# Routing of a mixture-of-experts layer: logits computed turned with the gate held in TensorE, and one-hot matrices built in bf16 for sixteen columns at once

## The chip, the cores and the metric

The kernel runs on one core of one Trainium2 chip. The metric is the device time of the whole program in microseconds (us), the median of repeated executions. TensorE (PE) multiplies, VectorE (DVE), ScalarE (ACT) and GpSimd (POOL) do the rest, SyncE (SP) issues most transfers.

## The reference

One macaron block over 4 × 1024 tokens of 256 channels, in float32:

```
x = x + 0.5 * ffn(layernorm(x))
x = x + attention(layernorm(x))      # 16 heads, RoPE, causal
x = x + 0.5 * ffn(layernorm(x))      # the same weights again

def ffn(x):                          # 4096 tokens, 8 experts, 2 of them for each token
    logits = x @ gate_w.T            # [4096, 8]
    top_w, sel = top_k(softmax(logits), 2); top_w /= sum(top_w)
    # each token: sum over its two experts of top_w * (silu(x @ w_gate[e]) * (x @ w_up[e])) @ w_down[e]
```

## The kernel before, in words

Everything runs in phases with a barrier between them: a setup, the first FFN (`ffn_phase`, tag f1), a projection phase, attention, an output phase, and `ffn_phase` again (tag f2). Each engine has one instruction list, written out by hand and run in order; semaphores are the only order between engines. The diff touches `ffn_phase` alone, and that runs twice. It has these stages.

**Logits stage.** The 4096 tokens are 32 tiles of 128. For each tile DVE normalises it (`normalise`, L386), SP stores it to DRAM (L312), PE turns it (two 128×128 transposes, `turn`, L567), ACT copies it out of PSUM (L520), and PE multiplies it with the gate (`logits`, L573): the turned tile is the stationary operand, and the eight columns of the gate move. `normalise(t)` needs the buffer of tile t−8, so it waits until that tile's store has landed (`xn_stored`) and until it is turned. In the same stage POOL splits the weights of the eight experts into a high and a low part (L336 to L341). Only two experts' raw weights fit, so SP, between two stores, waits for a split before it issues the next load: `load_weights(t // 5 + 2)` follows the store of tile 4, 9, 14, 19, 24 and 29, and waits until expert `t // 5` is split. The stores behind it in SP's queue wait with it.

**Choice and ranks.** DVE finds the two best experts of each token (`choose`, L401 to L405, and L409 between the two calls), PE counts tokens before each one, and DVE works out for each of the 8192 (token, choice) pairs a slot: a tile number `slot_j` (0 to 70) and a row `slot_p` (0 to 127).

**Inversion of the slots.** The experts need the reverse: which pair sits in a slot. The 8192 pairs are 64 columns of 128. For each column DVE writes a one-hot matrix of rows (L447, 128×128) and one of tiles times the pair number (L448, 128×71), both float32, and PE adds their product into `ps_owner` (L588), a float32 matmul that the chip runs as two passes. The buffers hold two lots of four columns. DVE then makes `pair_i` and `token_i` (L451 to L453), which release POOL's first gather, and a packed list of experts (L456 to L466), for which PE waits before the expert loop.

**Expert loop.** 71 tiles of 128 slots: gather by POOL, turn, gate and up, silu, down, scatter by POOL. After f2 the result is mixed into x and stored.

Of the kernel before, what the change touches and what calls it, by code (L numbers as in the profile page):

```python
# [18 lines left out]
BF16 = mybir.dt.bfloat16  # L19
# [13 lines left out]
SLOT_TILES = TOPK * NT + E - 1  # L33
DEEP = 8
# [10 lines left out]
                ("below", E), ("count", 128), ("pair1", TOPK * NT)]  # L45
# [6 lines left out]
def constants():  # L52
# [21 lines left out]
    put("pair1", TOPK * (P * np.arange(NT)[None, None, :] + p[:, None, None]) + np.arange(TOPK)[None, :, None] + 1)  # L74
# [83 lines left out]
def ffn_phase(nc, tag, cst, x_sb, rstd, nmr, w_mix, gate_sb, w_gate, w_up, w_down, xn_dram, y_dram, spare, out):  # L158
# [3 lines left out]
    with Semaphores(nc) as sems, ctx:  # L162
# [31 lines left out]
        xnT = carve(P, 4, KD, P)  # L194
# [28 lines left out]
        slot_j = sb("slot_j", [P, TOPK * NT])  # L223
        slot_p = sb("slot_p", [P, TOPK * NT])

        carved[0] = xnT_at
        at_row = carve(P, 2, 4, P)
        at_tile = carve(P, 2, 4, SLOT_TILES)
        empty = sb("empty", [P, SLOT_TILES])
        pair_i = sb("pair_i", [P, SLOT_TILES], I32)  # L230
# [33 lines left out]
        stats_own, moments = sem("stats_own"), sem("moments")  # L264
        xn_ready, xn_turned, xnT_ready, logits_done = sem("xn_ready"), sem("xn_turned"), sem("xnT_ready"), sem("logits_done")
# [111 lines left out]
        def _(dve):  # L377
# [3 lines left out]
            def normalise(t, u):  # L381
                if u == 0:
                    dve.wait_ge(moments, t // 8 + 1)
                wait(dve, xn_stored[u], 16 * (t // 8))
                wait(dve, xn_turned, t - 7)
                dve.tensor_scalar(xn[:, u, :], x_sb[:, t, :], rstd[:, t:t + 1], nmr[:, t:t + 1], ALU.mult, ALU.add).then_inc(xn_ready, 1)  # L386

            for t in range(NT):
                normalise(t, t % 8)
# [17 lines left out]
            dve.wait_ge(logits_done, NT)  # L407
# [34 lines left out]
            rows, tiles = cst("count"), cst("count")[:, 0:SLOT_TILES]  # L442
# [117 lines left out]
        def _(pe):  # L560
# [15 lines left out]
            for t in range(NT + 2):
                if t < NT:
                    turn(t)
                if t >= 2:
# [1054 lines left out]
```

## Time and profile before

| | |
|---|---|
| median of 3 runs | 1312.65 us (1310.78 to 1316.44) |
| the profiled execution | 1310.62 us, of which the span of its instructions is 1308.9 us |
| first FFN's logits stage | about 30.7 to 72.2 us |
| second FFN's logits stage | about 995.4 to 1037.2 us |
| second FFN: choice and ranks, inversion, expert loop and rest | 1037.2 to 1050.1, to 1078.3, to 1308.9 us |

Times in rows count from the first instruction. PEld is the weight load of TensorE, which overlaps PE. A duration on an engine holds a fixed latency that the next instruction may overlap, so what a stream costs is read from the distance of two starts. PEclk 1.00 is 2.4 GHz and 0.50 is 1.2 GHz.

### The profile page before, as it was taken

How to read it: one execution, taken by the hardware profiler on the slowest of the kernel's cores; microseconds unless marked ns; L12 is line 12 of the kernel's file. 1: busy time of each engine (PE TensorE's matmuls, PEld its weight loads, DVE VectorE, ACT ScalarE, POOL GpSimd, SP SyncE). 2: the span in 40 equal slices, each digit the busy share in tenths (PEclk: the TensorE clock that was granted, in tenths of full speed). 3: DMA queues.
4: the chain of work that ended last, by engine and by line, in shares of the span. 5: the costliest groups of instructions: out<-in, count | busy, mean ns of one | idle time of the engine just before them, and what ended most of it. 6: DMA issues, size and time to landing. Idle time of an engine off the chain costs nothing. (4 is left out here: it accounts for less than half of the span.)

```text
span 1308.9 us, 24181 instructions
## 1 busy us (share of the span) xinstructions
PE 1066.9 (82%) x6982; PEld 722.4 (55%) x6982; DVE 910.0 (70%) x2809; ACT 632.4 (48%) x1314; POOL 601.4 (46%) x757
## 2 busy tenths in 40 slices
PE   1958998890688659999999999999987788988850
PEld 1957987780576613333333333333286688977740
DVE  5787444444798768988999988898176894444436
ACT  1301555550576604666666666666762204555420
POOL 1923777773699801222222222222306707777750
PEclk9999999995799957999999999999986558999975
DMA  6611333321466531112111111100003402233339
GB/s 215 206 33 39 98 98 98 99 80 44 120 180 181 170 103 52 51 53 62 57 60 59 56 52 57 61 32 2 2 1 116 146 1 89 91 96 95 97 112 326
DMA packets 84077, 117.44 MB, mean 90 GB/s; under 512 B 11358, under 2 KB 64364, under 8 KB 80880
## 3 DMA queue, kind: packets, MB, share of 16 engines
q1 hardware_dynamic: 67200, 79.17, 19.3%
q0 software_dynamic: 13632, 33.59, 8.2%
q10 hardware_dynamic: 3120, 3.15, 0.7%
q8 instruction: 63, 1.03, 0.3%
q14 instruction: 62, 0.51, 0.1%
HBM read 75.48 MB, written 43.78 MB: 91 GB/s over the span
## 5 line engine op out<-in xcount | busy, mean ns | idle before, releaser
L1257 ACT ACTIVATE a_probs<-a_ps_s 128x1024 f32<-128x1024 f32 (+3 forms) x384 | 294.3, 813 | 173.1 <-PE a_ps_s L1289 171.9
L1172 POOL TENSOR_SCALAR_AFFINE_SELECT a_probs<-a_probs 128x256 f32<-128x256 f32 x256 | 102.5, 406 | 369.6 <-ACT a_probs L1257 366.9
L1190 DVE CUSTOM_DVE_ANT_0 a_unused<-a_ps_m,const_sb 128x128 bf16<-128x128 f32 (+3 forms) x512 | 234.1, 485 | 26.7 <-PE a_ps_m L1274 16.8
L1274 PE MATMUL a_ps_m<-st_k,st_q 96*128 96x512 bf16 (+3 forms) x768 | 219.7, 345 | 24.4 <-PEq L155 17.1
L354 POOL DMA_INDIRECT v_sb<-xn_dram,f_token_i x142 | 145.4, 1024 | 124.0 <-issue 80.5
L1192 DVE TENSOR_REDUCE a_max_a<-a_ps_m 128x1 f32<-128x512 f32 x256 | 175.7, 686 | 14.3 <-PE a_ps_m L1274 13.9
L1289 PE MATMUL a_ps_s<-st_q,st_k 98*128 98x512 bf16 (+3 forms) x768 | 180.8, 329 | 1.5 <-ACT a_probs L1257 1.4
L1274 PEld LDWEIGHTS a_ps_m<-st_k,st_q 96*128 96x128 bf16 x768 | 67.9, 98 | 196.6 <-DVE a_max_a L1192 55.9
L476 DVE TENSOR_TENSOR f_h<-f_ps_gu,f_sg 128x176 f32<-128x176 f32 x142 | 48.5, 341 | 175.3 <-ACT f_sg L537 175.3
L1302 PE MATMUL a_ps_ctx<-a_probs,a_v_st 128*32 128x512 f32 (+3 forms) x1536 | 163.7, 498 | 1.3 <-POOL a_probs L1172 0.6
L359 POOL DMA_INDIRECT y_dram<-v_sb,f_pair_i x142 | 143.5, 1011 | 43.5 <-issue 41.0
L1289 PEld LDWEIGHTS a_ps_s<-st_q,st_k 98*128 98x128 bf16 x768 | 65.4, 98 | 72.4 <-ACT a_probs L1257 42.6
L610 PE MATMUL f_ps_gu<-f_gu_hi,f_xT_hi 128*128 x284 | 95.9, 338 | 10.6 <-DVE f_xT_lo L471 9.8
L527 ACT ACTIVATE f_xT_hi<-f_ps_xT 128x256 fp32r<-128x256 f32 x142 | 53.6, 377 | 104.1 <-PE f_ps_xT L600 103.5
L628 PE MATMUL f_ps_y<-f_dn_hi,f_hT_hi 88*128 x284 | 92.9, 327 | 0.1
L610 PE MATMUL f_ps_gu<-f_gu_hi,f_xT_lo 128*128 x284 | 92.9, 327 | 0.0
L610 PE MATMUL f_ps_gu<-f_gu_lo,f_xT_hi 128*128 x284 | 92.9, 327 | 0.0
L537 ACT ACTIVATE f_sg<-f_ps_gu 128x176 f32<-128x176 f32 x142 | 45.0, 317 | 97.8 <-PE f_ps_gu L610 97.8
L600 PE MATMUL f_ps_xT<-const_sb,v_sb 128*128 128x128 f32 x284 | 59.2, 291 | 29.2 <-DMA v_sb<-xn_dram,f_token_i 28.9
L628 PE MATMUL f_ps_y<-f_dn_lo,f_hT_hi 88*128 x284 | 80.0, 282 | 0.0
L628 PE MATMUL f_ps_y<-f_dn_hi,f_hT_lo 88*128 x284 | 79.4, 280 | 0.0
L532 ACT ACTIVATE v_sb<-f_ps_y 128x256 f32<-128x256 f32 x142 | 54.6, 385 | 45.4 <-PE f_ps_y L628 45.4
(172 smaller groups left out, 2249.3 us busy)
## 6 DMA issues: line engine op xcount, KB each, us to landing
xn_dram<-v_sb SPq DMA_DIRECT2D x64, 128.0 KB, 3.4
p_yb<-y_dram SPq DMA_DIRECT2D x32, 256.0 KB, 2.8
v_sb<-y_dram SPq DMA_DIRECT2D x32, 256.0 KB, 3.8
st_q<-qk_dram SPq DMA_DIRECT2D x16, 384.0 KB
st_k<-qk_dram SPq DMA_DIRECT2D x16, 384.0 KB
qk_dram<-st_rT_hi SPq DMA_DIRECT2D x16, 256.0 KB, 2.9
qk_dram<-st_rT_mid SPq DMA_DIRECT2D x16, 256.0 KB, 3.5
qk_dram<-st_rT_lo SPq DMA_DIRECT2D x16, 256.0 KB, 5.1
```

The source lines that it names most:

```text
L354: pool.indirect_dma_start(xg[:, slot, :], None, xn_dram, bass.IndirectOffsetOnAxis(ap=token, axis=0), bounds_check=last_token, oob_is_err= ...
L359: pool.indirect_dma_start(y_dram, bass.IndirectOffsetOnAxis(ap=pair, axis=0), y_sb[:, slot, :], None, bounds_check=last_pair, oob_is_err=F ...
L600: mm = pe.transpose(ps_xT[b][:, k, :], xg[:, u, k * P:(k + 1) * P], ident)
L610: mm = pe.matmul(ps_gu[b][:, 0:2 * F], x_part[:, b, k, :], w_part[:, bass.ds(e, 1), k, :].rearrange("p a f -> p (a f)"), start=(n == 1), s ...
L628: mm = pe.matmul(ps_y[b][:], h_part[:, b, c, :], w_part[:, bass.ds(e, 1), c, :].rearrange("p a f -> p (a f)"), start=(n == 1), stop=(n == 6))
L1172: pool.affine_select(out=tri, in_=tri, compare_op=ALU.is_ge, fill=zero, base=0, pattern=[[0, 2], [1, P]], channel_multiplier=-1).then_inc( ...
L1190: dve.tensor_tensor_reduce(unused[:, bank, 0:nk], ps, cst("mask")[:, HALF - nk:HALF], 1.0, NEG, ALU.add, ALU.max, at).then_inc(taken, 1)
L1192: dve.tensor_reduce(at, ps, AX.X, ALU.max).then_inc(taken, 1)
L1257: act.activation(probs[:, s % 4, :, 0:nq], ps_s[s % 2][:, :, 0:nq], ACT.Exp, scale=float(HD) ** -0.5).then_inc(exp_done, 1)
L1274: pe.matmul(ps_m[bank][:, 0:nk], q_st[b][0:MAX_ROW, h, P * i:P * i + P], k_st[b][0:MAX_ROW, h, k0:k0 + nk], start=True, stop=True).then_in ...
L1289: mm = pe.matmul(ps_s[s % 2][:, n, 0:nq], k_st[b][:, h, P * j:P * j + P], q_st[b][:, h, q0:q0 + nq], start=True, stop=True)
L1302: mm = pe.matmul(ps_ctx[32 * h:32 * h + 32, q0 - HALF * half:HALF], v_st[b % 2][:, j, h, :], probs[:, (2 * v + h // 2) % 4, h % 2, 0:nq], ...
```

## The change

Three things. (1) `normalise` goes from DVE to ACT, and the copy of turned tiles from ACT to DVE; the gate becomes the stationary operand (128×8), four turned tiles (512 columns) move, DVE copies the 8×512 logits out of PSUM, and four small transposes bring them back to token rows. (2) The one-hot matrices are bf16 and built for sixteen columns by four DVE instructions, with a table `count_lot` that ACT writes once. (3) A pair number is no exact bf16 number, so the tile matrix has two halves of 71: 256 × tile number, and the low part; PE multiplies 142 columns in one bf16 pass, and one more DVE instruction adds the halves.

```
+LOT = 16
...
-        xnT = carve(P, 4, KD, P)
+        xnT = carve(P, 2, KD, 4 * P)
+        lgT = carve(E, 2, 4 * P)
...
+        count_lot = sb("count_lot", [P, P, LOT], BF16)
+        tile256 = sb("tile256", [P, TOPK * NT], BF16)
+        at_tile = sb("at_tile", [P, 2, 2 * SLOT_TILES, LOT], BF16)
-        at_row = carve(P, 2, 4, P)
-        at_tile = carve(P, 2, 4, SLOT_TILES)
+        at_row = carve(P, P * LOT).bitcast(BF16).rearrange("p (b s i) -> p b s i", b=2, s=P)
...
         @block.vector
-            def normalise(t, u):
...
+            def copy_turned(t):
+                i, u = t // 4, t % 4
+                dve.wait_ge(xn_turned, t + 1)
                 if u == 0:
+                    wait(dve, logits_done, i - 1)
+                dve.tensor_copy(xnT[:, i % 2, :, u * P:(u + 1) * P], ps_turn[u]).then_inc(xnT_ready, 1)
+
+            def copy_logits(i):
+                dve.wait_ge(logits_done, i + 1)
+                wait(dve, lg_ready, i - 1)
+                dve.tensor_copy(lgT[:, i % 2, :], ps_lgT[i % 2]).then_inc(lgT_ready, 1)
+
+            for i in range(NT // 4 + 1):
+                for u in range(4):
+                    if i < NT // 4:
+                        copy_turned(4 * i + u)
+                    if u == 1 and i > 0:
+                        copy_logits(i - 1)
...
-            for i in range(TOPK * NT):
-                b = i // 4 % 2
-                if i % 4 == 0:
-                    wait(dve, one_hot_used, i // 4 - 1)
-                dve.tensor_scalar(at_row[:, b, i % 4, :], rows, slot_p[:, i:i + 1], None, ALU.is_equal).then_inc(one_hot_ready, 1)
-                dve.tensor_scalar(at_tile[:, b, i % 4, :], tiles, slot_j[:, i:i + 1], cst("pair1")[:, i:i + 1],
-                                  ALU.is_equal, ALU.mult).then_inc(one_hot_ready, 1)
+            dve.wait_ge(count_ready, 2)
+            for lot in range(TOPK * NT // LOT):
+                b, of = lot % 2, slice(LOT * lot, LOT * (lot + 1))
+                hit, by_tile_no = at_tile[:, b, SLOT_TILES:2 * SLOT_TILES, :], at_tile[:, b, 0:SLOT_TILES, :]
+                per_tile = [P, SLOT_TILES, LOT]
+                wait(dve, one_hot_used, lot - 1)
+                own.then_wait(dve.tensor_tensor(hit, count_lot[:, 0:SLOT_TILES, :], slot_j[:, of].unsqueeze(1).to_broadcast(per_tile), ALU.is_equal))
+                own.then_wait(dve.tensor_tensor(by_tile_no, hit, tile256[:, of].unsqueeze(1).to_broadcast(per_tile), ALU.mult))
+                dve.tensor_scalar(hit, hit, cst("low")[:, LOT * lot // NT:LOT * lot // NT + 1], None, ALU.mult).then_inc(one_hot_ready, 1)
+                dve.tensor_tensor(at_row[:, b, :, :], count_lot[:], slot_p[:, of].unsqueeze(1).to_broadcast([P, P, LOT]),
+                                  ALU.is_equal).then_inc(one_hot_ready, 1)
...
+            own.then_wait(dve.tensor_tensor(pair_i[:], ps_owner[:, 0:SLOT_TILES], low[:], ALU.add))
...
         @block.scalar
+            def normalise(t, u):
+                if u == 0:
+                    act.wait_ge(moments, t // 8 + 1)
+                wait(act, xn_stored[u], 16 * (t // 8))
+                wait(act, xn_turned, t - 7)
+                act.activation(xn[:, u, :], x_sb[:, t, :], ACT.Identity, bias=nmr[:, t:t + 1], scale=rstd[:, t:t + 1]).then_inc(xn_ready, 1)
             for t in range(NT):
-                act.wait_ge(xn_turned, t + 1)
-                wait(act, logits_done, t - 3)
-                act.activation(xnT[:, t % 4, :, :], ps_turn[t % 4], ACT.Copy).then_inc(xnT_ready, 1)
+                normalise(t, t % 8)
+            act.activation(count_lot[:], cst("count").unsqueeze(2).to_broadcast([P, P, LOT]), ACT.Copy).then_inc(count_ready, 1)
+            act.activation(tile256[:], cst("tile256"), ACT.Copy).then_inc(count_ready, 1)
...
         @block.tensor
+            def logits(i):
+                pe.wait_ge(xnT_ready, 4 * i + 4)
+                wait(pe, lgT_ready, i - 1)
                 for k in range(KD):
+                    mm = pe.matmul(ps_lgT[i % 2], gate_sb[:, k, :], xnT[:, i % 2, k, :], start=(k == 0), stop=(k == KD - 1))
                 mm.then_inc(logits_done, 1)
+            def turn_back(i):
+                pe.wait_ge(lgT_ready, i + 1)
+                for u in range(4):
+                    mm = pe.transpose(ps_lg[:, 4 * i + u, :], lgT[:, i % 2, u * P:(u + 1) * P], ident[0:E, 0:E])
+                mm.then_inc(lg_ready, 1)
+
+            for i in range(NT // 4 + 2):
+                for u in range(4):
+                    if i < NT // 4:
+                        turn(4 * i + u)
+                    if u == 1 and 0 < i <= NT // 4:
+                        logits(i - 1)
+                if i >= 2:
+                    turn_back(i - 2)
...
             for i in range(TOPK * NT):
+                lot, b = i // LOT, i // LOT % 2
+                pe.wait_ge(one_hot_ready, 2 * lot + 2)
+                mm = pe.matmul(ps_owner, at_row[:, b, :, i % LOT], at_tile[:, b, :, i % LOT], start=(i == 0), stop=(i == TOPK * NT - 1))
```

## Rows read from the trace of the kernel before

**Rows 1.** The chain that ended last, in order of time, second FFN
```profile
1007.33 3.68 DMA xn_dram<-v_sb
...
1050.70 27.59 PE f_ps_y L588 x128
```

**Rows 2.** Stretches of both FFNs: length, busy of PE, PEld, DVE, ACT, POOL, PEclk, DMA
```profile
30.70:72.20 41.50, 38.58 (x192) 38.09 (x192) 29.06 (x34) 12.28 (x32) 38.36 (x37) 1.00 0.66 200
...
995.40:1037.20 41.80, 38.09 (x192) 37.85 (x192) 27.53 (x35) 12.29 (x32) 40.11 (x38) 0.50 0.65 199
1037.20:1050.10 12.90, 0.61 (x2) 0.13 (x2) 11.78 (x40) 0.23 (x1) 1.89 (x2) 0.50 0.00 0
1050.10:1078.30 28.20, 27.58 (x128) 27.38 (x128) 27.10 (x128) 0.00 (x0) 0.00 (x0) 0.50 0.00 1
```

**Rows 3.** Timeline of TensorE's weight loads in the second logits stage
```profile
1014.35 0.98 PEld L573 LDWEIGHTS f_ps_y<-gate_sb,v_sb 128*128 128x128 f32 x4
1015.06 0.48 PEld L567 LDWEIGHTS f_ps_hT<-const_sb,v_sb 128*128 128x128 f32 x2
1015.52 0.98 PEld L573 LDWEIGHTS f_ps_y<-gate_sb,v_sb 128*128 128x128 f32 x4
```

**Rows 4.** TensorE's instructions by form: count, busy us, mean ns, idle before
```profile
L1302 PE MATMUL a_ps_ctx<-a_probs,a_v_st 128*32 128x512 f32 x768 | 102.3, 604 | 0.3 <-ACT a_ctxT L1246 0.2
L1302 PE MATMUL a_ps_ctx<-a_probs,a_v_st 128*32 128x128 f32 x256 | 13.6, 285 | 0.4 <-POOL a_probs L1172 0.4
L583 PEld LDWEIGHTS f_ps_gu<-f_hot_sum,f_before_bf 128*128 128x128 bf16 x2 | 0.2, 106 | 13.3 <-DVE f_hot_sum L411 13.3
```

**Rows 5.** Granted clock around the second expert loop's start, and in the projection phase
```profile
1085.00:1090.00 5.00, 4.30 (x16) 3.95 (x15) 1.19 (x3) 2.37 (x4) 3.78 (x5) 0.50 0.32 95
1090.00:1095.00 5.00, 5.00 (x33) 4.82 (x32) 2.26 (x7) 2.72 (x9) 3.78 (x5) 0.82 0.29 83
365.00:375.00 10.00, 8.10 (x52) 6.82 (x50) 9.93 (x26) 6.89 (x17) 9.75 (x11) 1.00 0.73 200
```

**Rows 6.** Timeline of SP's queue, second FFN, and the landing of the stores
```profile
1019.49 0.38 SPq L304 DMA_DIRECT2D v_sb<-L_ffn_w_gate  x1
...
1020.90 3.55 SPq L312 DMA_DIRECT2D xn_dram<-v_sb  x5
...
DMA to landing us min/median/max: 1.7/3.4/4.9
```

**Rows 7.** Timeline of GpSimd, first and second FFN
```profile
72.92 1.26 POOL L341 TENSOR_TENSOR f_dn_lo<-v_sb,f_dn_hi 88x512 fp32r<-88x512 f32 x1
...
1018.21 1.26 POOL L341 TENSOR_TENSOR f_dn_lo<-v_sb,f_dn_hi 88x512 fp32r<-88x512 f32 x1
...
1037.29 1.80 POOL L347 MEMSET v_sb<- 128x2048 f32 x1
```

**Rows 8.** Timeline of VectorE, first and second FFN
```profile
72.23 0.42 DVE L401 TENSOR_REDUCE f_best<-f_ps_y 128x32 f32<-128x256 f32 x1 [3.74 <-PE f_ps_y L573]
...
73.15 1.31 DVE L403 TENSOR_TENSOR f_is_best<-f_is_best,const_sb 128x256 f32<-128x256 f32 x1
...
86.09 0.29 DVE L447 TENSOR_SCALAR v_sb<-const_sb,f_slot_p 128x128 f32<-128x128 f32 x1
...
1011.03 20.71 DVE L386 TENSOR_SCALAR v_sb<-x_sb,rstd,nmr 128x256 f32<-128x256 f32 x19 [6.34 <-DMA xn_dram<-v_sb]
```

**Rows 9.** Instructions of VectorE and ScalarE by form
```profile
L402 DVE TENSOR_TENSOR f_is_best<-f_others,f_best 128x256 f32<-128x256 f32 x2 | 0.8, 424 | 0.1
L456 DVE TENSOR_TENSOR f_work<-const_sb,f_first_tile 128x568 f32<-128x568 f32 x2 | 1.5, 742 | 0.0
L390 DVE CAST f_before_bf<-const_sb 128x128 bf16<-128x128 f32 x2 | 0.4, 214 | 0.0
L471 DVE TENSOR_TENSOR f_xT_lo<-f_ps_xT,f_xT_hi 128x256 fp32r<-128x256 f32 x142 | 59.1, 416 | 24.5 <-ACT f_xT_hi L527 24.4
L452 DVE SCALAR_TENSOR_TENSOR f_pair_i<-f_ps_y,f_empty 128x71 int32<-128x71 f32 x2 | 0.5, 232 | 0.1
L976 ACT ACTIVATE p_xn<-x_sb,nmr,rstd 128x256 f32<-128x256 f32 x32 | 19.0, 593 | 9.6 <-POOL nmr L887 9.6
```

More of the change, by code:

```diff
@@ L44 @@
 CONST_WIDTHS = [("ident", 128), ("before", 128), ("mask", 512), ("cos", NT * HD), ("sin", NT * HD),
-                ("below", E), ("count", 128), ("pair1", TOPK * NT)]
+                ("below", E), ("count", 128), ("tile256", TOPK * NT), ("low", TOPK)]
 CONST_AT = {}
@@ L73, in constants @@
     put("count", np.arange(128))
-    put("pair1", TOPK * (P * np.arange(NT)[None, None, :] + p[:, None, None]) + np.arange(TOPK)[None, :, None] + 1)
+    put("tile256", np.tile(TOPK * P * np.arange(NT), TOPK))
+    put("low", TOPK * p[:, None] + np.arange(TOPK)[None, :] + 1)
     return c
@@ L193, in ffn_phase @@
         xnT_at = carved[0]
-        xnT = carve(P, 4, KD, P)
+        xnT = carve(P, 2, KD, 4 * P)
+        lgT = carve(E, 2, 4 * P)
+        after_lgT = carved[0]
         best = sb("best", [P, TOPK, NT])
@@ L254, in ffn_phase @@
         ps_turn = [bank[:, :, :] for bank in ps_xT + ps_hT_bank]
+        ps_lgT = [bank[0:E, :] for bank in ps_gu]
         ps_lg = ps_y[0][:, 0:NT * E].rearrange("p (t e) -> p t e", e=E)
@@ L380, in _ @@
             own = Own(dve, dve_own)
-            def normalise(t, u):
+            def copy_turned(t):
+                i, u = t // 4, t % 4
+                dve.wait_ge(xn_turned, t + 1)
                 if u == 0:
[L383 to L389, printed above, removed]
+                    wait(dve, logits_done, i - 1)
[10 more added lines that the diff above has]
+                        copy_logits(i - 1)
             own.inc(dve.tensor_copy(before_bf[:], cst("before")))
@@ L450, in _ @@
             dve.wait_ge(owner_ready, 1)
-            own.then_wait(dve.tensor_scalar(empty[:], ps_owner, 0.0, EMPTY, ALU.is_equal, ALU.mult))
-            own.then_wait(dve.scalar_tensor_tensor(pair_i[:], ps_owner, -1.0, empty[:], ALU.add, ALU.add))
+            in_tile = ps_owner[:, SLOT_TILES:2 * SLOT_TILES]
+            own.then_wait(dve.tensor_scalar(empty[:], in_tile, 0.0, EMPTY, ALU.is_equal, ALU.mult))
+            own.then_wait(dve.scalar_tensor_tensor(low[:], in_tile, -1.0, empty[:], ALU.add, ALU.add))
@@ L453, in _ @@
+            own.then_wait(dve.tensor_tensor(pair_i[:], ps_owner[:, 0:SLOT_TILES], low[:], ALU.add))
             dve.tensor_scalar(token_i[:], pair_i[:], 1, None, ALU.logical_shift_right).then_inc(slots_ready, 1)
+            tiles = cst("count")[:, 0:SLOT_TILES]
             begun_j = work[:].rearrange("p (j e) -> p j e", e=E)
@@ L568, in turn @@
                 mm.then_inc(xn_turned, 1)
-            def logits(t):
-                pe.wait_ge(xnT_ready, t + 1)
+            def logits(i):
+                pe.wait_ge(xnT_ready, 4 * i + 4)
+                wait(pe, lgT_ready, i - 1)
                 for k in range(KD):
-                    mm = pe.matmul(ps_lg[:, t, :], xnT[:, t % 4, k, :], gate_sb[:, k, :], start=(k == 0), stop=(k == KD - 1))
+                    mm = pe.matmul(ps_lgT[i % 2], gate_sb[:, k, :], xnT[:, i % 2, k, :], start=(k == 0), stop=(k == KD - 1))
                 mm.then_inc(logits_done, 1)
[L576 to L579, printed above, removed]
-                    logits(t - 2)
+            def turn_back(i):
[11 more added lines that the diff above has]
+                    turn_back(i - 2)
             pe.wait_ge(hot_ready, 1)
@@ L586, in _ @@
             for i in range(TOPK * NT):
-                pe.wait_ge(one_hot_ready, 2 * i + 2)
-                mm = pe.matmul(ps_owner, at_row[:, i // 4 % 2, i % 4, :], at_tile[:, i // 4 % 2, i % 4, :],
-                               start=(i == 0), stop=(i == TOPK * NT - 1))
-                if i % 4 == 3:
+                lot, b = i // LOT, i // LOT % 2
+                pe.wait_ge(one_hot_ready, 2 * lot + 2)
+                mm = pe.matmul(ps_owner, at_row[:, b, :, i % LOT], at_tile[:, b, :, i % LOT], start=(i == 0), stop=(i == TOPK * NT - 1))
+                if i % LOT == LOT - 1:
                     mm.then_inc(one_hot_used if i < TOPK * NT - 1 else owner_ready, 1)
```

13 lines of the change are left out of this document (8 added, 5 removed).

## The prediction

> **What bounds the kernel now.** I read the chain that ended last first: in the second FFN it runs through the stores of normalised tiles and then through 27.59 us of the inversion's matmuls on PE without a break [rows 1]. The routing of an FFN hides behind nothing. A table of stretches gives its parts: logits stage 41.5 and 41.8 us, choice and ranks 12.9, inversion 28.2 [rows 2]. All that is won there is won in the span, twice; the barrier behind each FFN passes it on.
>
> In the logits stage PE is busy 38 of 41.8 us [rows 2]. Two turned tiles are 1.17 us apart (1014.35 to 1015.52), of which the four gate passes take 0.71 and the two transposes 0.46 [rows 3]; 32 × 1.17 = 37.4 us. That is at 1.2 GHz: the clock reads 0.50 in the second FFN [rows 2]. The first FFN's stage shows 1.00 but the same length and the same busy time for the same 192 matmul instructions, so I read it as 1.2 GHz too.
>
> Close behind PE stands a second limit: POOL splits weights for nearly the whole stage (40.1 us busy) [rows 2], and SP's stores are queued behind loads that wait for those splits.
>
> In the inversion PE and DVE are both full, 27.6 and 27.1 us of 28.2 [rows 2]: 0.42 us per column on each.
>
> **Part 1, the logits stage.** PE's work for four tiles becomes: 8 transposes, 4 passes of 512 float32 columns (2 halves of the channels × 2 passes), 4 small transposes. A 512-column pass at full clock: the 512-column form takes 604 ns and the 128-column form 285, so 384 columns cost 319 ns, 0.83 ns each, and 512 cost 0.43 us [rows 4]; at 1.2 GHz twice that, 0.85. The small transposes have no row; their nearest is an 8-column gate pass, 0.18 at 1.2 GHz [rows 3]; below, half of it. Then:
> - at 1.2 GHz: 4 × 0.46 + 4 × 0.85 + 4 × 0.18 = 5.96 us for four tiles, 47.7 for all, against 37.4 now. Slower.
> - at 2.4 GHz: 2.98 us, 23.8 for all.
>
> So the clock decides. What the engine did before it rose: at the second expert loop 352- and 256-column passes ran back to back from about 1086, and the clock went from 0.50 to 0.82 in the mean of the next 5 us [rows 5]. In the projection phase it is 1.00 while PE is busy 8.1 of 10 us [rows 5]. Streams of 8-column and 71-column passes stayed at 0.50 although busy throughout [rows 2]. The new stream is 512-column passes, 3.4 us of every 6, and transposes; I take it to be of the kind that rises after a lot or two, and keep the other as a rival.
>
> At full clock PE is no longer the limit; the stores are. The load behind store 19 waits for expert 3's split, which ends at 1018.21 + 1.26 = 1019.47, and is issued at 1019.49; with its two sisters SP is free for store 20 at 1020.90, then one store each 0.47 or so [rows 6, 7]. A store lands 3.4 us after issue [rows 6], and tile 28 needs store 20: it can be normalised at 1024.3, and tile 31, three stores later, at 1025.8. POOL does not get faster, so this date stays. ACT takes 0.59 for it, in place of DVE [rows 9]. Behind it: turn 0.5, DVE's copy 0.4 (a 256-column read of PSUM takes 0.42 [rows 9]), four passes 1.7 and their latency 0.2, the copy of 512 columns 0.7 (by the slope below), small transposes 0.6: 1030.6, say 1031, against 1037.2 now. **Gain 6 us**; in the first FFN the same reckoning gives 66.5 against 72.2 [rows 8], 5.7. ACT and DVE have cover: per four tiles ACT 4 × 0.59 and DVE 4 × 0.34 + 0.7, below 3 us. What is queued behind DVE's new waits is the copy of the next turned tile; PE needs it only a lot later. ACT's `count_lot` and `tile256` come behind tile 31, about 2 us, done long before the inversion.
>
> **What the gain runs into.** POOL goes on splitting until 1037.3 [rows 7]. Choice and ranks, now from 1031, falls under it. The trace shows the price once: L403, a two-input instruction, took 1.31 us at 73.15, when POOL's L341 ran until 74.18, against 0.42 for a like one alone [rows 7 to 9]. It ended right after POOL's instruction. Some six such DVE instructions now meet POOL's stream, whose pieces are 0.8 to 1.7 us. Bounds: nothing, or 6 × 0.9 = 5.4; I take 2 us, since an instruction in a gap passes. The first FFN already pays 0.9 of it. Net of part 1: slots are ready 4.6 us earlier in the first FFN (5.7 − 2 + 0.9) and 4.2 in the second.
>
> **Part 2, the inversion.** DVE per lot: two `tensor_tensor` of 71 × 16 = 1136, one `tensor_scalar` of 1136, one `tensor_tensor` of 2048, all operands bf16. The trace has no such instruction. In float32, 256 elements take 424 ns and 568 take 742: 163 ns and 1.02 per element [rows 9]. Upper bound, that rate per element: 1.32 + 1.32 + 1.32 + 2.25 and gaps and overlaps, 6.1 us per lot, 24.5 for four. Lower bound, by bytes, two bf16 elements at the cost of one float32: 0.74 + 0.74 + 0.74 + 1.21, less some overlap, 3.35 per lot, 13.4. The only row with bf16 in it, the cast of 128 elements, takes 214 ns where the float32 slope would give 294 [rows 9]; it is nearer to two elements per cycle, so I take 3.35. The `tensor_scalar` may be quicker still by 0.3.
>
> The Trainium skill (VectorE: DVE Perf Modes, "The perf-mode tier table") says that an all-bf16 `tensor_tensor` from SBUF runs at twice the float32 rate, 1224 against 2293 ns at 2048 elements, and a `tensor_scalar` at four times; no run here shows it yet. By it a lot would cost about 3.1 us.
>
> PE per column: a bf16 load of 128 columns, 106 ns at 1.2 GHz [rows 4], hidden by a pass of 142 columns, 142 / 1.2 = 118 ns (one column a cycle; by the float32 form above, a half of its two cycles): 0.13. Upper bound: today's 0.42. Sixteen columns 2.1 us, below DVE's 3.35, so only the last lot shows, 2.1 + 0.4 of hand-over. Sum 13.4 + 2.5 = 15.9 against 28.2: **gain 12.3 us** per FFN. One more instruction on 71 elements costs 0.26 (0.232 and a gap [rows 9]).
>
> **Sum.** First FFN 4.6 + 12.3 − 0.3 = 16.6, second 16.2, together 32.8. The profiled execution took 1310.6 (span 1308.9), which makes 1277.8; the median of the runs shown lies 2.0 higher, so 1280.
>
> **Rivals.**
> - *PE stays at 1.2 GHz in the logits stage.* For it: its level of 0.50 under streams that looked busy [rows 2]. Then the stage takes 47.7 + 3 us, 9 more than now; no meeting with POOL. Per FFN +9 (and −0.9 in the first) −12.3 + 0.3 = −3; two make −7: 1306. A clock that rises late lies between. Chance 0.17.
> - *bf16 gives DVE no second element*, for the small broadcast rows of 16. Inversion 24.5 + 2.5 = 27; gain 1.2, not 12.3: 1280 + 22 = 1302. Chance 0.08.
> - *PE reads columns 32 bytes apart* (`at_row[:, b, :, i % LOT]`), stationary and moving. No row shows such a read. At half rate 0.24 per column, 3.8 per lot, PE sets the pace: 3.4 + 4 × 3.8 = 18.6, 2.7 more per FFN: 1285, inside the forecast. The mechanism that ends on the other side: the read is slow and the load is no longer hidden, so that a column costs load and pass together. Now the inversion has 28.2 us and part 1 gives 4.1 net of the added instruction; less the first lot and the hand-over, (28.2 + 4.1 − 3.8) / 64 = 0.45 us per column is the point of no gain. It is (128 + 142) / 1.2 = 225 ns at half rate. At a third, 0.67, the inversion takes 46.6 and the kernel 1312.65 + 2 × 14.3 = 1341. Against it: loads are hidden behind passes elsewhere, PEld and PE being busy together [rows 2]. Chance 0.04.
> - *The change takes effect as forecast*, within 1268 to 1291: 0.71, the half-rate case in it.
>
> The Trainium skill speaks against the change here (SBUF — State Buffer, "Door 1", its note on cachelines): reads that cross to a new 16-byte line each element pay a penalty. By it the half-rate case would be the likely one, 1285. No row here shows its size.
>
> **Numbers.** 1280; its own range 1268 (no meeting with POOL, 4 us; `tensor_scalar` and passes quicker, 4; stores landing sooner, 4) to 1291. To hold 8 of 10 the range reaches up to 1304, over the bf16 case and the late clock. The least that a measurement of this kernel tells from no change is about 0.5%, 6.6 us, so faster means below 1306: 0.71 + 0.08 and most of the clock case, 0.88; same 0.08; slower 0.04.
>
> **What would show it.** Clock 1.00 in most of 1000 to 1031; normalising of tile 31 released by a store's landing; the first `choose` at about 66.5; L403-like instructions above 1 us beside POOL; four DVE instructions per lot near 0.74, 0.74, 0.7 and 1.2; PE idle between lots; inversion near 16 us. Wrong: clock 0.50 beside 512-column passes, 1.3 and 2.2 us for the DVE instructions, or PE without idle time in the inversion at 0.2 us or more per column.

## The result, and the profile after

The changed kernel takes 1290.93 us (median of 4 runs, 1289.48 to 1292.19) where the kernel before took 1313.91 in the same comparison (4 runs, 1310.78 to 1316.44). The ratio is 0.9827, 95% interval 0.9809 to 0.9845. A second comparison, on another chip, gave 0.9838 (0.9825 to 0.9852). The prediction was 1280; the time lies inside its range of 1268 to 1304, but the gain is 21 to 23 us where 33 were worked out. The question of this study is where the other 11 went.

The span of the profiled execution fell from 1308.9 to 1287.8 us. All stage lengths of this document are taken between the same events: the start of the phase's first GpSimd instruction, the first `choose`, the first one-hot instruction, the read of `ps_owner`. The first of them stands at 28.57 us before and at 27.98 changed.

| us | logits f1 | choice f1 | inversion f1 | logits f2 | choice f2 | inversion f2 | between the two | after the last |
|---|---|---|---|---|---|---|---|---|
| before | 43.66 | 13.86 | 28.19 | 43.97 | 12.95 | 28.19 | 878.93 | 230.58 |
| changed | 39.97 | 14.04 | 20.36 | 40.66 | 12.99 | 20.34 | 879.80 | 231.66 |

The table of stretches answers [rows 2]. Columns: stretch, its length, busy time and count of PE, PEld, DVE, ACT, POOL, PEclk, DMA share, GB/s. First logits stage, first inversion and second logits stage of the changed kernel:

```profile
27.98:67.95 39.97, 31.42 (x128) 12.24 (x128) 17.20 (x42) 18.44 (x34) 37.27 (x38) 0.91 0.72 214
...
81.99:102.35 20.36, 17.05 (x64) 9.37 (x64) 12.50 (x16) 0.00 (x0) 0.00 (x0) 0.50 0.00 0
982.10:1022.81 40.71, 31.15 (x128) 12.63 (x128) 17.36 (x43) 18.45 (x34) 38.27 (x39) 0.84 0.68 210
```

In the inversion DVE is down from 27.1 us to 12.5 (13.4 was worked out). PE has half the matmuls and is busy 17.05 us of 20.36. By form, over the first inversion (busy us, mean ns, idle before):

```profile
L632 PE MATMUL f_ps_y<-f_at_tile,v_sb 128*128 128x142 bf16 x64 | 17.1, 444 | 9.6 <-DVE v_sb L471 9.6
L632 PEld LDWEIGHTS f_ps_y<-f_at_tile,v_sb 128*128 128x128 bf16 x64 | 9.4, 148 | 17.2 <-DVE v_sb L471 10.1
L471 DVE TENSOR_TENSOR v_sb<-f_count_lot,f_slot_p 128x2048 bf16<-128x2048 bf16 x4 | 4.9, 1218 | 0.0
...
L468 DVE TENSOR_TENSOR f_at_tile<-f_count_lot,f_slot_j 128x1136 bf16<-128x1136 bf16 x4 | 3.0, 748 | 2.4 <-PE f_ps_y L632 2.4
L470 DVE TENSOR_SCALAR f_at_tile<-f_at_tile,const_sb 128x1136 bf16<-128x1136 bf16 x4 | 2.1, 516 | 0.1
```

Read the last column of L468: DVE, meant to be the slower side, waited 2.4 us for PE. And 17.05 / 64 = 0.266 us per column, twice the 0.13 of the sum. The chain that ended last shows the same in the second FFN, and answers to [rows 1]: what was 27.59 us of matmuls is

```profile
1039.08 17.04 PE f_ps_y L632 x64
```

In the logits stage PE's timeline answers to [rows 3]. The first FFN, around the place where it stands still:

```profile
45.84 0.69 PE L600 MATMUL f_ps_xT<-const_sb,v_sb 128*128 128x128 f32 x2 [4.27 <-ACT v_sb L548]
46.46 3.58 PE L607 MATMUL f_ps_gu<-v_sb,gate_sb 128*8 128x512 f32 x4
...
54.81 1.88 PE L607 MATMUL f_ps_gu<-v_sb,gate_sb 128*8 128x512 f32 x4
56.63 0.66 PE L600 MATMUL f_ps_hT<-const_sb,v_sb 128*128 128x128 f32 x4
57.22 0.41 PE L613 MATMUL f_ps_y<-const_sb,v_sb 8*128 8x8 f32 x4
57.56 0.66 PE L600 MATMUL f_ps_xT<-const_sb,v_sb 128*128 128x128 f32 x4
58.14 1.88 PE L607 MATMUL f_ps_gu<-v_sb,gate_sb 128*8 128x512 f32 x4
```

From start to start: four passes 1.82 us, four small transposes 0.34, eight transposes 1.17, together 3.33 for four tiles. After 45.84 PE doesn't wait again before the last lot. The stretches around the stop show the granted clock (last but two columns): it fell while PE stood still, and was at its lower level when PE came back.

```profile
40.00:43.00 3.00, 1.57 (x11) 0.94 (x10) 1.72 (x4) 0.00 (x0) 2.92 (x4) 1.00 0.52 144
43.00:46.00 3.00, 0.16 (x1) 0.16 (x2) 0.00 (x0) 0.81 (x2) 2.84 (x4) 0.52 0.82 268
46.00:48.00 2.00, 2.00 (x4) 0.37 (x5) 0.42 (x1) 1.75 (x4) 1.92 (x3) 0.50 1.00 285
```

From 50 to 52 us it reads 1.00 again. What held PE up stands in ACT's timeline, `normalise` of tile 13, which needs the buffer of tile 5:

```profile
45.19 2.56 ACT L548 ACTIVATE v_sb<-x_sb,nmr,rstd 128x256 f32<-128x256 f32 x5 [7.76 <-DMA xn_dram<-v_sb]
...
59.00 2.08 ACT L548 ACTIVATE v_sb<-x_sb,nmr,rstd 128x256 f32<-128x256 f32 x4 [1.36 <-DMA xn_dram<-v_sb]
60.98 1.89 ACT L552 ACTIVATE f_count_lot<-const_sb 128x2048 bf16<-128x2048 f32 x1
```

Store 5 stands in SP's queue behind the load that waits for expert 0's split; the load is issued at 40.15 and store 5 at 41.56:

```profile
40.15 0.38 SPq L315 DMA_DIRECT2D v_sb<-L_ffn_w_gate  x1
...
41.56 2.33 SPq L323 DMA_DIRECT2D xn_dram<-v_sb  x5
```

### The profile page after: what moved, and what is told of

Its sections match the earlier page's. It is cut to its first block and busy times, and to the rows that moved or that the text cites. A ratio compares the mean times of both kernels' runs of the same rounds, so it can differ in the third digit from the quotient of the medians.

```text
span 1287.8 us, 23449 instructions
## 1 busy us (share of the span) xinstructions
PE 1033.1 (80%) x6726; PEld 635.5 (49%) x6726; DVE 859.6 (67%) x2603; ACT 644.9 (50%) x1318; POOL 601.2 (47%) x757
## 5 line engine op out<-in xcount | busy, mean ns | idle before, releaser
L1233 DVE CUSTOM_DVE_ANT_0 a_unused<-a_ps_m,const_sb 128x128 bf16<-128x128 f32 (+3 forms) x512 | 234.2, 485 | 27.1 <-PE a_ps_m L1317 17.0
L653 PE MATMUL f_ps_gu<-f_gu_hi,f_xT_hi 128*128 x284 | 96.0, 338 | 11.4 <-DVE f_xT_lo L497 10.7
```

Of the source, the lines that this page charges most:

```text
L653: mm = pe.matmul(ps_gu[b][:, 0:2 * F], x_part[:, b, k, :], w_part[:, bass.ds(e, 1), k, :].rearrange("p a f -> p (a f)"), start=(n == 1), s ...
L1233: dve.tensor_tensor_reduce(unused[:, bank, 0:nk], ps, cst("mask")[:, HALF - nk:HALF], 1.0, NEG, ALU.add, ALU.max, at).then_inc(taken, 1)
```

## The experiments

Two theories stood against each other for the inversion. A: PE reads an operand whose elements lie 32 bytes apart at half rate, or less. B: the load of the weights is not hidden, and a column costs load and pass together (0.147 + 0.12 = 0.27 would fit as well). For the logits stage the question was whether PE's pace or the early wait for stores is worth more.

The first four runs were made on one chip on which the kernel before took 1381.93 us. In the three of them without extra matmuls the stretch between the two routings and the one after the second took 34 to 38 us longer than in the table above, while the routing stages had their usual lengths. So these runs are compared with one another.

**pe_steps_b.** Behind the inversion, seven blocks of 32 bf16 matmuls of 142 columns into a buffer that is free then; the steps of the stationary and of the moving operand are 32/32, 2/32, 32/2, 2/2, 16/16, 8/8 and 4/4 bytes. The rest of the kernel is as changed.

```
+            def every(flat, n, step, i):
+                return flat[:, 0:n * step].rearrange("p (s i) -> p s i", i=step)[:, :, i % step]
+            for i in range(N):
+                pe.matmul(ps_gu[0][:, 0:n2], every(row_flat, P, 16, i), every(tile_flat, n2, 16, i), start=True, stop=True)
...
```

> The changed kernel, and behind each inversion PE runs 7 blocks of 32 extra bf16 matmuls (128-column load, 142-column pass) over the same buffers into a PSUM bank that is free then; the output stays the reference's. The blocks differ in the step between the elements that PE reads, stationary / moving: 32 B / 32 B, 2 B / 32 B, 32 B / 2 B, 2 B / 2 B, then 16 B, 8 B and 4 B for both. In the changed kernel a column costs 0.266 us. Theory A (the step slows the read): 0.27, then a lower value when the operand that matters is contiguous, and 0.12 to 0.15 with both contiguous; with 8 B and 4 B near the contiguous value. Rival B (a bf16 pass behind its own weight load costs that anyway at 1.2 GHz, 106 + 118 ns and an overhead, not overlapped): 0.22 to 0.27 in all seven blocks.

PE's timeline in the first FFN, each line a block, in the order above:

```profile
101.89 8.58 PE L642 MATMUL f_ps_gu<-f_at_tile,v_sb 128*128 128x142 bf16 x32
110.29 8.41 PE L644 MATMUL f_ps_gu<-f_at_tile,v_sb 128*128 128x142 bf16 x32
118.52 3.96 PE L646 MATMUL f_ps_gu<-f_at_tile,v_sb 128*128 128x142 bf16 x32
122.28 2.60 PE L648 MATMUL f_ps_gu<-f_at_tile,v_sb 128*128 128x142 bf16 x32
124.72 8.40 PE L650 MATMUL f_ps_gu<-f_at_tile,v_sb 128*128 128x142 bf16 x32
132.94 4.33 PE L652 MATMUL f_ps_gu<-f_at_tile,v_sb 128*128 128x142 bf16 x32
137.09 2.30 PE L654 MATMUL f_ps_gu<-f_at_tile,v_sb 128*128 128x142 bf16 x32
```

By the distance of the starts: 0.262 us per matmul with both operands at 32 bytes, 0.257 with only the moving one, 0.118 with only the stationary one, 0.076 with neither (the clock rose in that block). At clock 0.50 the stationary step costs nothing that can be seen, the moving one is the whole price, and theory B falls. Both at 16 bytes cost 0.257, at 8 bytes 0.130, at 4 bytes 0.067. The second FFN's blocks repeat all but the contiguous one (0.072) within 0.001. The stretches show at which clock (last but two columns; the first is the inversion itself, both operands at 32 bytes):

```profile
85.00:101.90 16.90, 16.83 (x65) 9.44 (x66) 9.38 (x13) 0.00 (x0) 0.00 (x0) 0.50 0.00 1
118.52:122.20 3.68, 3.68 (x33) 3.68 (x32) 0.00 (x0) 0.00 (x0) 0.00 (x0) 0.50 0.00 0
124.72:132.90 8.18, 8.18 (x35) 4.63 (x33) 0.00 (x0) 0.00 (x0) 0.00 (x0) 0.83 0.00 0
132.94:137.00 4.06, 4.06 (x33) 3.92 (x32) 0.00 (x0) 0.00 (x0) 0.00 (x0) 0.51 0.00 0
137.09:139.20 2.11, 2.11 (x34) 2.11 (x32) 0.00 (x0) 0.00 (x0) 0.00 (x0) 1.00 0.00 0
```

The slow read costs 0.257 at a mean clock of 0.83 and 0.262 at 0.50: 1.8 ns per column whatever the clock, so a faster clock would not have helped the inversion. Within the block of 16 bytes the clock reads 1.00 until 130 us and 0.50 from 131 on, and stretches of 1 us from 126 on hold 5 to 6 of its matmuls at either level. At 1.2 GHz 142 columns take 0.118, and 8 bytes are a tenth above that; what 8 bytes cost at 2.4 GHz isn't shown.

The Trainium skill (Advanced Engine Details and Errata, "SBUF Cachelines") says that at least two hits on a 16-byte line are needed for full rate. The blocks agree: one element in each line is slow at 16 and at 32 bytes alike, two in a line take 0.130 us where the contiguous rate at 1.2 GHz is 0.118. The page gives no size, and doesn't say that the stationary operand is spared.

**inversion_only_b and logits_only_b.** Each is the kernel before with one half of the change: the one-hot matrices and the two-part counts alone, or the turned logits with the moved `normalise` and copy alone.

```
 inversion_only: + count_lot, at_tile, at_row in bf16, LOT = 16; normalise on DVE, gate passes of one tile, as before
 logits_only:    + xnT of four tiles, copy_logits, turn_back; one-hot columns one by one in float32, as before
```

> The logits stage of before (normalise on DVE, copies on ACT, tile as the stationary operand) with the new bf16 inversion. If the two parts add up: 2 x (7.8 - 0.3) = 15 us less than before, about 1298. If the new logits stage is what leaves room for the inversion or takes from it, the time differs from that by more than 2 us.

> The new logits stage with the float32 inversion of before. If the parts add up: 3.7 + 3.3 less, about 1306 to 1307. If the meeting of the choice with GpSimd's splits costs what the prediction said (2 us a time), 1309.

The ratios to before are 0.9884 (0.9842 to 0.9927) and 0.9934 (0.991 to 0.9958): −16.4 and −8.7 us, 25 together, each with an interval of several us (10 to 22, and 6 to 12), so this sum can't be told from the 21 to 23 of the whole change, which wasn't run on this chip. The stages are those of the whole change (inversion 20.34 and 20.36; logits 40.37 and 40.36), and in this the halves don't help or hinder each other.

**lot8_b.** `LOT = 8`: the step of both operands becomes 16 bytes, DVE does eight lots of half the size.

```
-LOT = 16
+LOT = 8
```

> LOT = 8: eight columns per lot, so PE reads every 16 bytes instead of every 32, and the first lot and the last are half as long. By theory A with a penalty that stays as long as each element lies in another 16-byte line: still 0.266 per column, 17.0 us of PE, first lot 1.9 instead of 3.3: 1.3 us less per FFN, 2 to 3 us less than the changed kernel, 1288. By a penalty that shrinks with the step: 0.2 per column, 13 us, then DVE sets the pace with 8 x 1.9 = 15: 4 us less per FFN, 1283. By rival B: as the first.

Ratio 0.9831 (0.9788 to 0.9874), the changed kernel's. The inversion takes 19.23 us, 1.1 less, about what a first lot of half the size saves; PE's price stayed (17.19 us for 64 columns), as the 16-byte block says.

**tile_by_four.** The direct test of theory A in the kernel: the tile matrix, the moving operand, is written in groups of four columns, so that its elements lie 8 bytes apart. DVE writes as many bytes by as many instructions; the rows stay at 32.

```
-        at_tile = sb("at_tile", [P, 2, 2 * SLOT_TILES, LOT], BF16)
+        at_tile = sb("at_tile", [P, 2, LOT // FOUR, 2 * SLOT_TILES, FOUR], BF16)
...
-                mm = pe.matmul(ps_owner, at_row[:, b, :, i % LOT], at_tile[:, b, :, i % LOT], start=(i == 0), stop=(i == TOPK * NT - 1))
+                mm = pe.matmul(ps_owner, at_row[:, b, :, i % LOT], at_tile[:, b, i % LOT // FOUR, :, i % FOUR], start=(i == 0), stop=(i == TOPK * NT - 1))
```

> The changed kernel with the tile matrix laid out in groups of four columns, so that PE's moving operand is read every 8 bytes and not every 32; the row matrix, the stationary operand, stays at 32 bytes; the instructions of DVE are as many and as large. Theory A from the block measurement (the moving step alone costs, 0.26 at 32 and 16 bytes, 0.13 at 8): 0.12 to 0.13 us per column, a lot of 16 takes PE 2.1 us, DVE sets the pace with 3.13 a lot: 4 x 3.13 + 2.1 + 0.4 = 15.0 against 20.4 us, 5.4 us less per FFN, 10.7 less than the changed kernel. If DVE loses its two elements per cycle on rows of four (rival): about 6 us a lot, 26 us, 11 more than the changed kernel.

It ran beside the changed kernel under the name changed_again, and two more:

> The changed kernel itself, on the chip of the three runs below, as their point of reference. 21 to 25 us less than before.

1277.06 against 1289.7 us; ratio to before 0.9741 (0.9727 to 0.9755) against 0.9838 (0.9825 to 0.9852). The inversions take 15.05 and 15.03 us where 15.0 were expected. PE's timeline (the last of four lots) and DVE's first instruction behind it:

```profile
94.25 2.35 PE L637 MATMUL f_ps_y<-f_at_tile,v_sb 128*128 128x142 bf16 x16 [0.79 <-DVE v_sb L476]
```

```profile
96.63 0.23 DVE L480 TENSOR_SCALAR f_empty<-f_ps_y 128x71 f32<-128x71 f32 x1 [2.44 <-PE f_ps_y L637]
```

This is the picture that the prediction drew: PE idle between lots, released by DVE, and 2.44 us for the last lot. Of the 12.6 us between the two times, where 10.7 were expected, the two inversions account for 10.6, which is more than the 8.9 by which they had missed the forecast of 15.9 each.

**stores_first.** The loads of the weights are moved behind later stores, so that no early store waits for a split.

```
+LOAD_AFTER = [14, 20, 27, 31, 31, 31]
...
-                if t % 5 == 4 and t // 5 + 2 < E:
-                    load_weights(t // 5 + 2)
+                for e, after in enumerate(LOAD_AFTER):
+                    if t == after:
+                        load_weights(e + 2)
```

> The changed kernel with SP's loads of the raw weights 2 to 7 behind the stores of tiles 14, 20, 27, 31, 31, 31 in place of 4, 9, 14, 19, 24, 29. Theory: PE's wait for tile 13 (41.6 to 45.8 us) came from stores queued behind a load that waits for GpSimd, and the clock fell in it, so that the next four passes took 3.58 instead of 1.88 us. Without it the logits stage ends 4.2 + 1.7 = 5.9 us earlier; the choice then lies wholly beside GpSimd's splits. If the meeting costs what the changed kernel showed (0.2 us more than before), 10 to 12 us less than the changed kernel; if it costs the 2 us of the prediction, or more, 8 or less. Rival: the stage is bound by PE's passes at 3.3 us for four tiles, and the wait only moves the same work: under 3 us in all.

The logits stage took 33.27 and 33.13 us instead of 39.64 and 40.50 in the run beside it: the early wait and the clock's fall behind it are worth 6.4 and 7.4 us, and the stage ran at clock 1.00 from 31 us to its end. But only 4.2 us reached the time: 1285.49, ratio 0.9805 (0.9792 to 0.9818). The choice took 18.2 us in both FFNs. DVE's timeline, where GpSimd splits the last two experts until 72.07, and GpSimd's memset behind them:

```profile
61.76 1.00 DVE L425 TENSOR_TENSOR f_is_best<-f_is_best,const_sb 128x256 f32<-128x256 f32 x1
...
66.78 1.08 DVE L427 TENSOR_TENSOR f_hot<-const_sb,f_chosen 128x256 f32<-128x256 f32 x1
...
68.58 1.65 DVE L434 TENSOR_TENSOR f_gap<-f_best 128x32 f32<-128x32 f32 x1
...
71.19 2.66 DVE L438 TENSOR_SCALAR w_mix<-f_gap 128x32 f32<-128x32 f32 x1
...
72.13 2.09 DVE L444 TENSOR_TENSOR_SCAN f_running<-f_ones_bf,f_ps_gu 128x32 f32<-128x32 bf16 x8
```

```profile
72.01 1.80 POOL L360 MEMSET v_sb<- 128x2048 f32 x1
```

Alone the same five take 0.42, 0.59, 0.18, 0.18 and 0.99. The price that the prediction read from one instruction [rows 7, 8] and called a meeting is 5 us once the choice lies wholly beside GpSimd's work. The splits are not the only such work. DVE's last two instructions here end just behind GpSimd's memset of `v_sb` (72.01 to 73.81): from L438 to L446 DVE takes 3.06 us where it takes 1.21 alone, so some 1.9 of the 5 us are the memset's. In the changed kernel the memset (72.39 to 74.19) lies beside `tensor_tensor` and `tensor_reduce` instructions of the choice, and holds none of them up: they take their 0.42 and 0.59.

**both_mended.** tile_by_four and stores_first together.

> The edits of tile_by_four and stores_first together. They touch different stages, so they should add up: about 19 to 22 us less than the changed kernel.

1277.51 us, ratio 0.9739 (0.9726 to 0.9753): nothing over tile_by_four. Logits 32.74 and 32.47, but choice 19.00 in both. The expectation that the two gains add was wrong. The stages don't account for all of it: in the profiled execution the six routing stages are 4.2 us shorter than tile_by_four's, but that execution is the fastest of five (1273.39 us, the others 1276.87 to 1277.99), and where the rest of the median's time lies isn't shown.

**splits_paused and paused_four.** To see whether it is the neighbourhood of GpSimd, and not the earlier start, that makes the choice long, GpSimd pauses before expert 6 until the first lot of one-hot columns is written; with the moving operand at 32 bytes, and at 8.

```
+                if e == PAUSE_AT:
+                    pool.wait_ge(one_hot_ready, 2)
```

> stores_first (1285.5 beside 1311.3 and 1289.7), in which the choice, 18.2 us instead of 14.0 in the first FFN, lies beside GpSimd's splits. Here GpSimd waits before the split of expert 6 until VectorE has built the first lot of one-hot matrices, so two of eight experts are split beside the inversion, where PE sets the pace and DVE has about 1 us of idle time per lot. Theory (SBUF's shared port, or whatever it is that GpSimd's two-input work holds up, cost the 4 to 5 us): the choice returns to about 13 us, the inversion stays within 1 us of 20.4, and the kernel takes 6 to 9 us less than stores_first. Rival (the choice got longer for another reason, such as transfers in flight): the choice stays near 18 us and the time within 2 us.

> The same with the tile matrix in groups of four (both_mended, 1277.5). DVE sets the pace of the inversion now, so the splits beside it are no longer free: if they hold DVE up as they did the choice, the inversion takes 18 to 19 us instead of 15 and the kernel 2 to 5 us less than both_mended; if the bf16 instructions pass between GpSimd's, 7 to 9 less.

The choice is back at 13.28 and 13.53 us in the one and 13.00 and 13.54 in the other. The cost moved along with the work: the inversion takes 23.73 in the first and 21.64 in the second, where 20.3 and 15.04 are the undisturbed lengths. The times are 1281.79 (ratio 0.9765, 0.9742 to 0.9789) and 1277.44 (0.9731, 0.9711 to 0.9751). The second gained nothing over both_mended. The first did gain: its ratio is 0.4% below that of stores_first and the intervals don't overlap, some 5 us where 6 to 9 were expected, though on another chip. Its inversions grew by 3.4 us each and those of paused_four by 6.6, which fits that DVE has idle time beside PE's slow read and none beside the fast one; but "within 1 us of 20.4", as expected, it was not. In splits_paused both engines suffer. DVE, then GpSimd, in the same stretch:

```profile
78.69 1.20 DVE L474 TENSOR_TENSOR f_at_tile<-f_at_tile,f_tile 128x1136 bf16<-128x1136 bf16 x1
79.93 1.82 DVE L475 TENSOR_SCALAR f_at_tile<-f_at_tile,const_sb 128x1136 bf16<-128x1136 bf16 x1
81.67 1.63 DVE L476 TENSOR_TENSOR v_sb<-f_count_lot,f_slot_p 128x2048 bf16<-128x2048 bf16 x1
83.22 1.82 DVE L473 TENSOR_TENSOR f_at_tile<-f_count_lot,f_slot_j 128x1136 bf16<-128x1136 bf16 x1
```

```profile
78.06 1.23 POOL L352 CAST f_gu_hi<-v_sb 128x704 fp32r<-128x704 f32 x1 [15.19 <-DVE v_sb L476]
79.37 2.06 POOL L353 TENSOR_TENSOR f_gu_lo<-v_sb,f_gu_hi 128x704 fp32r<-128x704 f32 x1
81.38 0.84 POOL L356 CAST f_dn_hi<-v_sb 88x512 fp32r<-88x512 f32 x1
82.30 2.14 POOL L357 TENSOR_TENSOR f_dn_lo<-v_sb,f_dn_hi 88x512 fp32r<-88x512 f32 x1
```

The four DVE instructions take 0.75, 0.52, 1.22 and 0.75 alone, and the `tensor_scalar` with one tensor input grows most, 0.52 to 1.82. GpSimd's pieces take 0.77, 1.67, 0.60 and 1.26 alone. The two lists run as if in turns: DVE's four instructions take 6.4 us (78.69 to 85.08 from start to start) and GpSimd's four 6.3 (78.06 to 84.39), in place of 3.1 and 4.4.

The Trainium skill (SBUF — State Buffer, "SBUF: two separate sides") says that VectorE and GpSimd take turns at a shared port pair, held by one of them for a whole instruction when VectorE's has two SBUF inputs or runs in a two-port mode. These rows agree with that in kind; the page gives no price for a stream of such instructions, and the rows don't show the port itself.

**high_by_scalar_first.** If GpSimd's presence is the price, less of its work should bring the price down. ScalarE makes the high parts of the weights and GpSimd only the subtractions; tile_by_four and a late order of the loads are kept.

```
+LOAD_AFTER = [10, 15, 20, 24, 28, 31]
+HIGH_AFTER = [7, 11, 19, 23, 27, 31, 31, 31]
...
+            def high(e):
+                act.wait_ge(gu_in[e % 2], 32 * (e // 2 + 1))
+                act.activation(gu_hi[:, e, :, :], gu_raw[:, e % 2, :, :], ACT.Copy).then_inc(high_made, 1)
+                act.wait_ge(dn_in[e % 2], 16 * (e // 2 + 1))
+                act.activation(dn_hi[:, e, :, :], dn_raw[:, e % 2, :, :], ACT.Copy).then_inc(high_made, 1)
...
-                own.then_wait(pool.tensor_copy(gu_hi[:, e, :, :], gu_raw[:, e % 2, :, :]))
+                pool.wait_ge(high_made, 2 * e + 1)
```

> Beside both_mended, two things change: ScalarE makes the bf16 high parts of the split weights (two copies of 0.9 and 0.5 us or so per expert) and GpSimd keeps only the subtractions, about 3.0 us per expert where both took 4.4; and the weight loads are placed a little earlier. Theory: the choice takes 19 us instead of 13 to 14 because GpSimd's splits of the last experts lie beside it, and with less of them the splits end near 65 us of the span instead of 72. Then logits stay near 33 us, the choice takes about 15 instead of 19, the inversion stays at 15.0, and the kernel takes 4 to 9 us less than both_mended did: 0.967 to 0.970 of before. Rival: the slowdown follows the subtractions, which have two inputs and stay on GpSimd, or ScalarE's added 1.4 us per expert hold up its normalising: the choice stays at 18 to 19 or the logits stage grows, and the time is within 2 us of both_mended or above it.

1268.99 us, ratio 0.9688 (0.9669 to 0.9706), the fastest kernel of the study. Its stages in the first FFN (stretches: logits, choice, inversion), and under them the first two of both_mended:

```profile
27.60:61.41 33.81, 29.55 (x128) 12.06 (x128) 17.10 (x42) 24.94 (x46) 25.53 (x22) 1.00 0.79 243
61.41:76.05 14.64, 0.61 (x2) 0.13 (x2) 13.48 (x41) 3.48 (x5) 7.33 (x5) 0.58 0.07 22
76.05:91.10 15.05, 9.36 (x64) 8.21 (x64) 12.34 (x17) 0.00 (x0) 0.00 (x0) 0.50 0.01 2
```

```profile
27.80:60.50 32.70, 28.46 (x128) 11.98 (x128) 17.09 (x42) 18.34 (x34) 29.89 (x31) 1.00 0.75 235
60.50:79.50 19.00, 0.61 (x2) 0.13 (x2) 17.82 (x41) 0.23 (x1) 14.24 (x12) 0.53 0.15 45
```

GpSimd works 7.33 us beside the choice instead of 14.24, and the choice takes 14.64 instead of 19.00 (second FFN 15.35 instead of 19.00). Not all of these 4.4 us are owed to less work: in both_mended a `tensor_scalar` of 8 elements met the memset and took 1.99 us in place of 0.17, which held DVE up by 1.5 us, and here the memset begins earlier, at 67.15, and meets no such instruction. Of the two ratios, 0.9688 and 0.9739, the difference is 6.7 us of 1311, inside the 4 to 9 expected; the two ran on different chips, each beside the kernel before, and differ in the order of the loads too.

**high_by_scalar.** The same move of the high parts, with the loads in the order of the changed kernel.

> The same move of the high parts to ScalarE, with the stores in the order of the changed kernel (experiment tile_by_four with this one edit). Theory: the stores of the normalised tiles keep GpSimd's pace of one expert's split, 4.4 us with both parts and about 3.5 without the high ones, so the logits stage takes 37 to 39 us instead of 40.3 and the choice 13.0 to 13.5, with the inversion at 15.0: 2 to 6 us less than tile_by_four, 0.969 to 0.972 of before. Rival: ScalarE gives back in its own queue what GpSimd gains, or TensorE's pace sets the logits stage anyway: logits at 40 us or more and the time within 2 us of tile_by_four or above it.

1277.32 us, ratio 0.9742 (0.9721 to 0.9764): tile_by_four's, and the rival's case. The wait for tile 13 fell from 4.27 to 2.35 us, as meant, but the logits stage took 41.46 and 37.98 us (tile_by_four 40.23 and 40.26). PE's timeline:

```profile
43.74 0.69 PE L613 MATMUL f_ps_xT<-const_sb,v_sb 128*128 128x128 f32 x2 [2.35 <-ACT v_sb L552]
44.36 3.58 PE L620 MATMUL f_ps_gu<-v_sb,gate_sb 128*8 128x512 f32 x4
...
50.49 3.12 PE L620 MATMUL f_ps_gu<-v_sb,gate_sb 128*8 128x512 f32 x4
```

The passes at 50.49 still took 3.12 us for four, where the changed kernel's at 51.49 took 1.88. In the first FFN that took more than the shorter wait gave. Why the clock came back later after a shorter stop isn't settled.

## Why the prediction was right, and where its numbers were not

**The inversion on DVE: right.** The steps were 0.74, 0.74, some 0.7 with a note that it may be 0.3 quicker, and 1.21; measured are 0.75, 0.75, 0.52 and 1.22, and a lot every 3.13 us where nothing disturbs it; [rows 9] had no such form. The rival that bf16 gives no second element is refuted.

**The inversion on PE: the term that was mis-sized.** The sum took 0.13 us per column; measured is 0.266. The half-rate read was among the rivals, with 0.24 per column, 18.6 us for the inversion and 1285 for the kernel, and it happened, a little dearer: 20.36. It is 4.5 us per FFN over the 15.9 of the sum, 8.9 of the 11.7 us that the span fell short. The rival's step "stationary and moving" is half wrong: only the moving operand pays (pe_steps_b), and its graver form, load and pass together, is refuted by the block with the moving operand contiguous. The row from which 0.13 was worked out, [rows 4], has contiguous operands, and can't say anything on a step; the half-rate value and the upper bound stood in the text, and 0.13 was chosen below them without a row of a strided read.

**The logits stage: right in kind, 2.0 and 2.9 us short.** The clock rose as forecast: 0.91 and 0.84 in the mean, and the passes took 0.45 us where 0.43 was worked out. The date at which the last tile can be normalised was right: 32.6 us after the phase's start by the prediction (1025.8 − 993.2). By the trace the last four are normalised from 59.00 to 60.98, a store's landing releases the first, and the last begins at about 60.5, 32.5 us after 27.98. The step "at full clock PE is no longer the limit" failed. PE was behind that date, for three reasons that the prediction didn't sum: it stood still 4.27 us (second FFN 5.24) for tile 13, because the first such wait of SP's queue matters as well as the last; it came back at the lower clock, 3.58 us for four passes; and four tiles cost 3.33, not 2.98, of which the transposes are 0.25 (0.147 each and not 0.115). stores_first takes the stop and the clock's fall away, and the stage is 6.4 and 7.4 us shorter, so these two are shown; the third, the pace of four tiles, is read from the rows alone.

**The meeting with GpSimd: over-priced here, under-priced as a mechanism.** 2 us per FFN were put down. Against the undisturbed 12.95, the choice took 14.04 and 12.99 us, 1.1 and 0. This gave back 2.9 us of the sum, because the stage ended later than forecast. With the choice wholly beside the splits it costs 5 to 6 us (18.2 and 19.0), about the upper bound of the prediction, 5.4. It also explains why a shorter logits stage alone brings little: its end runs into the same work of GpSimd, whose end stays at 72 to 73 us. That the price follows GpSimd's work to another place is shown by the paused kernels; high_by_scalar_first agrees that it falls with less of that work, but 1.5 of its 4.4 us come from where the memset happened to lie.

**The sum again.** Of 32.8 us forecast, 21.1 came in the span. The inversion fell short by 8.9, the logits stages by 4.9, the choice gave back 2.9. The remaining 0.8 lies outside the six stages: before the first, between the two routings and after the second the changed kernel takes 1.36 us more in all (−0.59, +0.87, +1.08), of which 0.6 was put down for the added instructions. The time came out at 1290.93, at the very edge of the 1268 to 1291 that the prediction gave to "takes effect as forecast"; without the 2.9 us that the late end of the stage gave back it would have lain beyond it (though inside 1304), and that was luck.

**Rivals.** PE staying at 1.2 GHz in the logits stage did not happen. In the first FFN's first microseconds the clock reads 1.00 (30.81 to 31.80 us) while four transposes take 1.18 us, the duration of the lower level, as at 1004.18 with 1.12 behind a stop. This speaks for reading the first stage of the kernel before as 1.2 GHz in spite of its 1.00 [rows 2], but it wasn't tested.

## What to carry to other kernels

If an operand is laid out for a fast elementwise engine, price how TensorE will read it: for bf16 at 1.2 GHz a moving operand with 8 bytes from element to element kept nearly the full rate and one with 16 did not, and the large step cost nothing on the stationary one. A stage that a faster engine shortens moves the next one beside whatever still runs; here that was GpSimd. Over tile_by_four neither taking the wait from PE (both_mended) nor taking work from GpSimd (high_by_scalar) brought anything alone; the two together brought 0.5%. Where a queue mixes loads that wait with stores that others wait for, follow the first such wait as well as the last: here TensorE came back from a stop of 4.27 us at half its clock.

## What the runs showed of the hardware

- A bf16 moving operand with one element in each 16 bytes costs 1.8 ns per column at either clock; the stationary operand at 32 bytes costs nothing that can be seen (0.118 us for 142 columns at clock 0.50).
- bf16 `tensor_tensor` with an operand that repeats the same sixteen, or the same four, values runs at two elements for each float32 one: 1136 elements in 0.75 us, 2048 in 1.22.
- Beside each other, DVE's long instructions take 1.3 to 3.5 times as long (one with one tensor input too, 0.52 to 1.82 us), a short one of 32 elements up to 1.65 us in place of 0.18, and GpSimd's 1.2 to 1.7 times.
- GpSimd's memset, which reads nothing, held up a short `tensor_scalar` until its own end (2.66 us in place of 0.18 in stores_first, 1.99 in place of 0.17 in both_mended, in both FFNs of each), while the choice's `tensor_tensor` and `tensor_reduce` instructions beside it in the changed kernel took their usual time.
- A shorter stop of TensorE does not always cost less (one execution each): after 2.35 us passes were slow still at 50.49, 6.1 us after the first; after 4.27 us they were fast at 51.49, 5.0 us after the first.
